# The first tile of a pairwise product kernel, with its rows laid in memory in another order

## The reference

```python
vid = jnp.einsum('bfd,de->bfe', x, W)
idx_i, idx_j = jnp.triu_indices(F_, k=1)
return x[:, idx_i, :] * vid[:, idx_j, :]
```

## Time and profile before

| | us |
|---|---|
| median of 3 runs | 1283.99 |
| lowest and highest run | 1283.84, 1284.1 |
| span of the profiled execution | 1282.9 |
| VectorE busy in it | 1079.9 |
| TensorE busy in it | 184.4 |

### The profile page before, as it was taken

One profiled execution on the slowest core, in us unless ns is written; L12 is line 12 of the kernel. 1 busy time (PEld: TensorE's weight loads), 2 busy tenths in 40 slices (PEclk: granted clock), 3 DMA queues, 4 the chain that ended last, 5 costly groups with the idle time before them and its releaser, 6 DMA issues. The chain is left out here.

```text
span 1282.9 us, 1255 instructions
## 1 busy us (share of the span) xinstructions
PE 184.4 (14%) x256; PEld 71.9 (6%) x256; DVE 1079.9 (84%) x273; POOL 0.2 (0%) x4
## 2 busy tenths in 40 slices
PE   2012110302111030300020211103020030202100
PEld 1000000100000010100010000001010010100000
DVE  6589989988897989998028989989998899899980
POOL 0000000000000000000000000000000000000000
PEclk7555565655655565655565565656565565655655
DMA  9999999999999999999999999999999999999999
GB/s 406 424 427 438 435 433 435 443 431 427 437 438 433 425 437 434 436 429 445 418 419 427 436 430 436 438 438 424 440 439 429 432 435 439 425 439 439 431 423 409
DMA packets 11810, 553.70 MB, mean 432 GB/s; under 512 B 1312, under 2 KB 1312, under 8 KB 1312
## 3 DMA queue, kind: packets, MB, share of 16 engines
q1 hardware_dynamic: 6048, 277.38, 50.1%
q10 hardware_dynamic: 5760, 276.30, 49.9%
HBM read 33.59 MB, written 520.09 MB: 432 GB/s over the span
## 5 line engine op out<-in xcount | busy, mean ns | idle before, releaser
L295 DVE TENSOR_TENSOR mem<-mem,vid 128x1024 f32<-128x1024 f32 (+11 forms) x270 | 1079.3, 4065 | 161.5 <-DMA out_dram<-mem 113.2
L315 PE MATMUL vid<-mem,w 128*128 x256 | 184.4, 888 | 1010.2 <-PEq L313 1010.2
L315 PEld LDWEIGHTS vid<-mem,w 128*128 128x128 f32 x256 | 71.9, 295 | 1121.9 <-issue 1121.9
L226 DVE COPY w<-mem 64x64 f32<-64x64 f32 x2 | 0.4, 189 | 5.0 <-DMA mem<-in_r_x_dram 4.9
L223 DVE MEMSET w<- 128x128 f32 x1 | 0.2, 165 | 0.8 <-PEq L340 0.8
L340 POOL MEMSET const-bfloat16-1.0<- 128x1 bf16 x1 | 0.1, 102 | 0.0
L340 POOL MEMSET const-uint8-127<- 128x1 uint8 x1 | 0.1, 102 | 0.0
L340 POOL MEMSET const-float32-0.0<- 128x1 f32 x1 | 0.1, 98 | 0.2 <-issue 0.2
L340 POOL MEMSET const-float32-1.0<- 128x1 f32 x1 | 0.1, 98 | 0.0
## 6 DMA issues: line engine op xcount, KB each, us to landing
out_dram<-mem SPq DMA_DIRECT2D x9, 7680.0 KB, 23.3
out_dram<-mem ACTq DMA_DIRECT2D x3, 7680.0 KB, 23.1
out_dram<-mem SPq DMA_DIRECT2D x3, 7168.0 KB, 21.6
out_dram<-mem ACTq DMA_DIRECT2D x3, 5120.0 KB, 17.5
out_dram<-mem ACTq DMA_DIRECT2D x2, 7168.0 KB, 22.6
out_dram<-mem ACTq DMA_DIRECT2D x2, 6656.0 KB, 21.4
out_dram<-mem SPq DMA_DIRECT2D x2, 6656.0 KB, 19.8
out_dram<-mem ACTq DMA_DIRECT2D x3, 4096.0 KB, 17.5
```

The lines of the kernel that those rows point to most:

```text
L226: lambda: nc.vector.tensor_copy(w2[half, half], mem[half, place + F, :D]),
L295: lambda: nc.vector.tensor_tensor(o, left, right, ALU.mult),
L315: last = nc.tensor.matmul(vid[:, b : b + BANK, :], lhsT=w2[:, :], rhs=xt(b), start=True, stop=True)
```

## The change

Row 8e + k of `x0` (e from 0 to 15, k from 0 to 7) is stored by the host at place 16k + e. The two transfers of tile 0 read the array through a pattern that undoes this, so that partition 8e + k still gets row 8e + k. Bytes, destinations, waits and queues stay as they are. The source pattern now has the dimensions 16, 8 and the run, where it had 128 and the run. The rows e = 0 to 15 for one k lie next to each other in memory.

```diff
     place = place_of(0, F)
+    rows = x0.rearrange("(k e) u c -> e k (u c)", e=P // 8)
     first = [
         transfer(
             mem[:, :, :].rearrange("p u c -> p (u c)")[:, (place + HALF) * C : (place + F) * C + D],
-            x0.rearrange("p u c -> p (u c)")[:, HALF * C : F * C + D],
+            rows[:, :, HALF * C : F * C + D],
             (place + HALF, place + F + 1), False, [],
         ),
-        transfer(mem[:, place : place + HALF, :], x0[:, :HALF, :], (place, place + HALF), False, []),
+        transfer(
+            mem[:, :, :].rearrange("p u c -> p (u c)")[:, place * C : (place + HALF) * C],
+            rows[:, :, : HALF * C],
+            (place, place + HALF), False, [],
+        ),
     ]
...
     x0[:, F, :D] = _np.concatenate([w, w])
+    x0 = x0.reshape(P // 8, 8, *x0.shape[1:]).swapaxes(0, 1).reshape(x0.shape)
```

## The result

The changed kernel takes 1288.64 us (median; 1288.4 to 1288.74), the kernel before 1284.07 us on the same chip: a ratio of 1.0033, 95% interval 1.0023 to 1.0043. It is 4.6 us slower. The profiled spans differ by about as much, 1287.4 against 1282.9 us.

A forecast was written before the change was run, and what follows sets the result against it. The prediction took the DMA stream at 434 GB/s to bound the kernel. Its terms, 0.0 (host) + 0.0 (decoding) - 0.2 us (first step), took 1283.99 us to 1283.8 us, range 1283.0 to 1288.8 us.

The forecast's parts named there:

- Rival A: Two transfers of tile 0: engines share ways into on-chip memory, half rate, 5.0 us lost, 1288.8 us; chance 0.25.
- What bounds the kernel: Whole span: the DMA stream at 434 GB/s; vector or tensor work is free, lost stream time paid in full.
- steps 4 and 5: Start: products' landing changes hidden, cover 16 us; rest: full stream, so changes in first microseconds pass one to one.
- step 4: First products: landing changes cost nothing; sign: first-store wait stays 14.88 us but for its start's move against the stores.
- Step 2: The two transfers: same bytes, places and pieces; only source-pattern decoding might cost, taken as 0.0, range 0.0 to 0.3 us.
- step 3: Slow first step, 1.70 to 3.00 us: nearer rows gain 0.2 us, bounds -0.62 and +0.62 us.
- likeliest case: Whole kernel: no change within 0.2%, chance 0.72, own range 1283.2 to 1284.9 us.

The follow-up runs named there:

- destination probes: Against the changed kernel, first transfer made 64 partitions from 16 x 4 source rows, aimed at different first partitions; kernels took 1285.6 to 1291.46 us, times not compared.
- shape without the order: Against the changed kernel, x0 in natural row order with one unused row behind every eight, source pattern still 16 x 8: 1288.88 us, ratio to before 1.0035.
- 32 x 4 kernels: Against the changed kernel, source pattern 32 x 4, once with neighbouring rows, once in natural order with an unused row behind every four: both 1284.98 us, ratios 1.0005.
- Half of the change: Against the changed kernel, only the first transfer keeps 16 x 8 permuted rows; the second reads a natural-order copy by 128 rows: 1286.32 us, ratio 1.0013.
- all loads: Against the changed kernel, x permuted like x0 and all eight loads, 33.59 MB, read by 16 x 8 patterns: 1364.62 us, ratio 1.0626.
- probes at 32, 0 and 28: First transfer of 64 partitions, 16 x 4 source rows, to partitions from 32, 0 or 28, against the changed kernel: landed in 5.2, 7.6 and 7.1 us.
- probe at 16: The same 64-partition first transfer aimed at partitions 16 to 79, against the changed kernel: landed in 7.8 us; whole kernel 1291.46 us, one execution.

## Why the prediction was wrong

The forecast was 1283.8 us and no change that could be measured; 1288.64 us came, inside the range of 1283.0 to 1288.8 but slower by 0.33%, clear of the scatter. Rival A, with a chance of 0.25, gave 1288.8 us and is what happened.

**What bounds the kernel** was right: vector and tensor time is free, stream time is paid in full. The first store moved by 4.51 us, the last by 4.47, the span by 4.5, and the first product's 2.45 us cost nothing (steps 4 and 5). One sign that step 4 was given didn't come as said: the vector engine's wait for the first store should have grown by what the store moved against the products, 4.51 - 2.45 = 2.06 us, and grew by 0.54. The first store's issue is 4.51 us later, but it landed 16.0 instead of 17.5 us after its issue.

**Step 2 failed.** It took the edit to leave the two transfers alone but for the decoding, as bytes, pieces and destinations stay. It gave no price to what the shape decides, which engine writes which partitions, and step 3 let both transfers run at the full rate behind their first step. The rate of 426 GB/s in rows 7 belongs to the shape of 128 rows, and I carried it over to 16 x 8 in the forecast. The destination probes (5.2 against 7.6 us) and the shape without the order (1288.88 us) show the sharing in its place; it cost 4.1 to 4.3 us, against the 0.62 us at which step 3 bounded a loss. The decoding was taken at 0 of a range of 0 to 0.3 us. SP's first issue took 0.27 us more, within that, but the first byte came about 0.4 us later, also in the 32 x 4 kernels, where nothing moved before 2.10 us either; their first loads landed 5.4 and 5.3 us after the issue, against 5.1.

**Step 3** had the place right and the effect wrong. A slow first step exists, but a full-rate transfer in either order gives the same 1284.98 us, and there the first step moved 149 and 130 GB/s, against 188 before (0.4 of its 1.3 us now pass before the first byte). Of the 0.2 us taken as a gain nothing could be measured. Yet nearer rows do seem to be read sooner: the first sixteen packets took 0.44 us (median) with neighbouring rows and 0.82 us with rows far apart where the source is 16 x 8, and 0.77 and 0.93 us where it is 32 x 4, in one trace each. Nothing of it reached the end: in the two 32 x 4 traces the fourth load is complete at 38.54 us with neighbouring rows and at 38.44 us without.

**Rival A's own working** held in the main: 5.0 us expected for the sharing, 4.1 to 4.3 measured. The two transfers ran at 262 and 222 GB/s, not at 213 throughout, and the first step, slow already, lost little (169 against 188 GB/s). That its total came within 0.2 us of the measured time is partly luck: the term was too large by about 0.8 us, the late first byte wasn't in it, and it was added to 1283.8 us, which holds a gain that didn't come. The lower end of the likeliest case's range has the same slip: 1283.2 us takes the bound of 0.62 us off the forecast of 1283.8, while the upper end adds to 1283.99. Half of the change cost 2.1 us, all loads 80.4 us against 79. The map of the Trainium skill on which rival A leaned (page "SBUF — State Buffer", section "Door 1: The DMA port swizzle") is borne out by the probes at 32, 0 and 28, and not by the 266 GB/s of the probe at 16; where they differ the measurement stands. The mistake was in the weights. Against A I set only that no present row shows a slow load, and a row of the old shape can't speak about the new one.

## What to carry to other kernels

A transfer's access pattern decides not only which bytes move but, as the probes imply, which engine moves them; changing the outermost dimension of one side can halve the rate of a transfer with the same bytes, pieces and destinations. So before a pattern is reshaped, ask which partitions each engine will then write, and read the rate of that transfer in a table by stage, not only the page: over the span this loss is 432 against 430 GB/s. In a kernel whose stream is never idle, every such microsecond is paid at the end, however far away that is.

## What the runs showed of the hardware

- With 128 partitions as destination, a source of 16 x 8 rows ran at 222 to 262 GB/s, one of 32 x 4 at up to 437 and one of 64 x 2 at up to 432. That 32 and 64 keep the split of 128 rows, and that 16 gives each engine eight partitions in a row, is my reading of these rates; the trace doesn't name the engine of a packet.
- Engines held to half the rate count as busy: the DMA share was 1.04 at 222 GB/s, and 0.96 over 62 us at 199 GB/s. A full DMA row doesn't mean a full rate.
- Transfers of 64 partitions landed 5.2, 7.1, 7.6 or 7.8 us after their issue by their first partition alone (32, 28, 0, 16), in one execution each. At 28, fourteen of the sixteen increments of its semaphore came by 5.90 us and two at 7.65 and 7.79 us.
- With a three-dimensional source pattern on the first transfer SP's first issue took 0.63 to 0.67 us instead of 0.38, and the first byte came about 0.4 us later.
